# Layer-norm statistics from accumulators: row sums where the residuals are written, squares in one pass of ScalarE

## The reference

```
def _layernorm(x, axis=-1, eps=1e-05):
    m = jnp.mean(x, axis=axis, keepdims=True)
    v = jnp.var(x, axis=axis, keepdims=True)
    return (x - m) / jnp.sqrt(v + eps)

x = x + _L0_xattn_ref(_layernorm(x), ctx, ctx)        # autocorrelation by FFT, 9 best lags
x = x + _L0_ffn_ref(_layernorm(x), ...)               # dense 1024x1024 + low-rank experts, 2 of 8
x = x + _L1_xattn_ref(_layernorm(x), ctx, ...)        # windowed attention, 8 heads, window 16
x = x + _L1_ffn_ref(_layernorm(x), ...)               # low-rank experts, 2 of 4
```

## Time and profile before

| | |
|---|---|
| time, median of 3 runs | 2359.71 us (2359.32 to 2360.57) |
| span of the profiled execution | 2357.6 us |
| what lies around the span (median less span) | 2.1 us |
| busy: PE, DVE, ACT, POOL | 84%, 85%, 53%, 42% of the span |
| granted clock of TensorE, mean | 0.918 of full speed |

### The profile page before, as it was taken

How to read it: one execution, slowest core, us unless ns; L and a number is a source line. 1 busy time by engine, 2 the same in 40 slices (tenths; PEclk the granted TensorE clock), 3 DMA queues, 4 the chain that set the end, 5 groups by cost and what they waited for, 6 DMA issues and landing times.

```text
span 2357.6 us, 50630 instructions
## 1 busy us (share of the span) xinstructions
PE 1982.8 (84%) x18912; PEld 1159.5 (49%) x18912; DVE 2012.7 (85%) x5613; ACT 1246.3 (53%) x1795; POOL 994.9 (42%) x582
## 2 busy tenths in 40 slices
PE   5688888988888988888888888888888898888875
PEld 2355444555544555544555544555544555544543
DVE  5788889888889888898888898888888988898863
ACT  3255555455555455554555555455555555555543
POOL 1354434344434434444435444435434435434431
PEclk7899999999999999999999999999999999999985
DMA  5011110011110010111010111011111011111000
GB/s 195 10 37 37 45 44 31 22 44 36 44 44 35 18 44 36 44 44 40 13 44 36 44 44 44 9 44 36 44 44 44 9 44 36 44 44 36 9 10 19
DMA packets 24735, 91.58 MB, mean 39 GB/s; under 512 B 3137, under 2 KB 3265, under 8 KB 24577
## 3 DMA queue, kind: packets, MB, share of 16 engines
q1 hardware_dynamic: 24704, 91.17, 10.9%
HBM read 74.39 MB, written 16.78 MB: 39 GB/s over the span
## 4 chain that ended last, share of the span: by engine, by line
PE 38%; DVE 25%; issue 17%; ACT 10%; POOL 9%; DMA 0%; DVEq 0%; POOLq 0%; SPq 0%; ACTq 0%
PE pa L433 12%; PE pb L433 5%; PE pb L531 4%; PE pc L626 4%; PE pc L600 3%; POOL p_hl L1366 3%; POOL rest L1354 3%; POOL sc L1409 3%; DVE small L1118 2%; PE pc L433 2%; PE pb L536 2%; ACT v_pad L770 2%; DVE small L935 2%; DVE sc L1070 2%; DVE sc L1139 2%
## 5 line engine op out<-in xcount | busy, mean ns | idle before, releaser
L531 PE MATMUL pb<-w_base_h,even_words 128*128 128x512 f16 x1024 | 341.1, 396 | 0.4 <-ACT mid_t L712 0.4
L1409 POOL TENSOR_TENSOR sc<-sc,sc_rec 128x512 f32<-128x512 f32 x128 | 134.1, 1047 | 349.7 <-DVE sc_rec L1148 349.7
L1359 POOL TENSOR_TENSOR rest<-rest,v_im 128x1024 f32<-128x1024 f32 x32 | 75.6, 2363 | 453.4 <-DVE v_im L1031 453.4
L1366 POOL TENSOR_TENSOR p_hl<-sc,p_hl 128x512 f16<-128x512 f32 x128 | 191.1, 1493 | 161.6 <-ACT p_hl L712 161.6
L433 PE MATMUL pa<-ctx_a,tab 128*128 128x512 f32 x384 | 243.0, 767 | 16.8 <-DMA par<-in_parity 8.4
L433 PE MATMUL pa<-xn_a,tab 128*128 128x512 f32 x384 | 189.4, 617 | 43.4 <-ACT xn_a L712 43.4
L804 ACT ACTIVATE q_diag<-sc,par 32x1024 f32<-32x1024 f32 x192 | 215.9, 1140 | 9.7 <-DVE sc L1070 7.4
L600 PE MATMUL pc<-sc_t,v_diag 128*128 128x32 f16 x6144 | 174.0, 177 | 54.6 <-ACT rows_c L712 54.6
L600 PEld LDWEIGHTS pc<-sc_t,v_diag 128*128 128x128 f16 x6144 | 168.1, 97 | 89.5 <-ACT rows_c L712 60.5
L531 PE MATMUL pb<-w_base_l,even_words 128*128 128x512 f16 x512 | 201.2, 393 | 0.0
L712 ACT ACTIVATE rows_c<-pc 64x256 f32<-64x256 f32 x256 | 96.2, 376 | 183.9 <-PE pc L600 180.8
(11 more groups left out here) (141 smaller groups left out, 5357.8 us busy)
## 6 DMA issues: line engine op xcount, KB each, us to landing
x_a<-in_x SPq DMA_DIRECT2D x32, 512.0 KB, 3.3
ctx_a<-in_ctx_in SPq DMA_DIRECT2D x32, 512.0 KB, 3.3
x_res<-in_x SPq DMA_DIRECT2D x32, 512.0 KB, 3.9
ctx_b<-in_ctx_in SPq DMA_DIRECT2D x32, 512.0 KB, 4.1
out<-rows_c SPq DMA_DIRECT2D x32, 512.0 KB, 2.9
v_diag<-in_base_w SPq DMA_DIRECT2D x1, 4096.0 KB, 14.3
tab<-in_spectra SPq DMA_DIRECT2D x1, 576.0 KB, 5.1
q_diag<-in_ra SPq DMA_DIRECT2D x1, 544.0 KB, 15.2
```

The source lines that it names most:

```text
L531: mm(pb[:, h, :], rows[:, cols], weights[:, j, h * HALF:(h + 1) * HALF], start=(j == 0 and m == 0), stop=False)
L1366: g_.tensor_tensor(part[:, :, :, LO], sc[:, g % 2, :, :], part[:, :, :, HI], ALU.subtract)\
L1409: g_.tensor_tensor(sc[:, g % 2, :, :], sc[:, g % 2, :, :], sc_rec[:, blocks].unsqueeze(2).to_broadcast([P, GB, KEYS]), ALU.mult)\
```

## The change

Norm 0 keeps `bn_stats` and `bn_aggr`. For norms 1, 2 and 3 the operation that writes the residual also accumulates the sum of each row (for norm 1 a tensor_tensor becomes a scalar_tensor_tensor for that). VectorE turns that sum into the mean (`mean`, one 128x1 operation). ScalarE gets a new operation, `spread`: Square over all 1024 columns with the row sum as bias and a scale of -D, so that it squares (sum - D x), and an accumulator output that is D^2 times the sum of squared deviations. Its elementwise result goes to the place that the normalised rows will overwrite (xn_b or xn_c) and is not used. `root` k = 0 then waits for ScalarE (`ln_sq`) and not for VectorE's own `ln_mv`. The six `bn_stats` and three `bn_aggr` of these norms go. A memset of 128x1, with which the kernel holds back an operation of VectorE until a semaphore has come, goes before each of the three `bn_aggr` too.

```
+            def spread(b, n, rows, rows_out, place):
...
+                act.wait_ge(rows_out.sem, rows_out.after(b))
+                nc.scalar.activation(place[:, :], rows[:, :], ACT.Square, bias=ln_sum[n][:, :], scale=-float(D),
+                                     accum_out=mv[n][:, 1:2]).then_inc(ln_sq[n].sem, 1)
...
                     c_attended(c, 3)
+                if do_b:
+                    spread(b, 2, x_b, x2_out, xn_b)
                 if do_a:
                     a_values_long(i, 1)
...
                     a_transposed(i, 0)
                     a_transposed(i, 1)
+                if do_c:
+                    spread(c, 3, rows_c, x3_out, xn_c)
                 if do_b:
                     b_values(b)
...
                     b_value_blocks(b, 0, 1)
+                if do_a:
+                    spread(i, 1, x_b, x1_out, xn_b)
+                if do_b:
                     b_value_blocks(b, 0, 2)
...
+            def mean(b, n, rows_out):
+
+                dve.wait_ge(rows_out.sem, rows_out.after(b))
+                v.tensor_scalar(mv[n][:, 0:1], ln_sum[n][:, :], 1.0 / D, None, ALU.mult).then_inc(ln_mean[n].sem, 1)
...
                 if k == 0:
-                    dve.wait_ge(ln_mv[n].sem, ln_mv[n].after(b))
-                    v.tensor_scalar(var, mv[n][:, 1:2], 1e-5, 4.0 * RSQRT_K ** 6, ALU.add, ALU.mult)\
-                        .then_inc(steps.sem, 1)
+                    dve.wait_ge(ln_sq[n].sem, ln_sq[n].after(b))
+                    v.tensor_scalar(var, mv[n][:, 1:2], 4.0 * RSQRT_K ** 6 / D ** 3, 1e-5 * 4.0 * RSQRT_K ** 6,
+                                    ALU.mult, ALU.add).then_inc(steps.sem, 1)
...
-                v.tensor_tensor(x_b[:, :], pa_lo, x_res[:, :], ALU.add).then_inc(x1_out.sem, 1)
-
-
-            def b_norm(b, n, before):
-                dve.wait_ge(before.sem, before.after(b))
-                layer_norm(b, n, x_b)
+                v.scalar_tensor_tensor(out=x_b[:, :], in0=pa_lo, scalar=1.0, in1=x_res[:, :], op0=ALU.mult,
+                                       op1=ALU.add, accum_out=ln_sum[1][:, :]).then_inc(x1_out.sem, 1)
...
-                                       op0=ALU.mult, op1=ALU.add).then_inc(x2_out.sem, 1)
+                                       op0=ALU.mult, op1=ALU.add, accum_out=ln_sum[2][:, :]).then_inc(x2_out.sem, 1)
...
-                                       op0=ALU.add, op1=ALU.add).then_inc(x3_out.sem, 1)
-
-            def c_norm(b):
-                dve.wait_ge(x3_out.sem, x3_out.after(b))
-                layer_norm(b, 3, rows_c)
+                                       op0=ALU.add, op1=ALU.add, accum_out=ln_sum[3][:, :]).then_inc(x3_out.sem, 1)
...
                 if do_b:
-                    b_norm(b, 1, x1_out)
-                    variance(b, 1)
+                    mean(b, 1, x1_out)
...
                     b_base(b)
-                    b_norm(b, 2, x2_out)
-                    variance(b, 2)
+                    mean(b, 2, x2_out)
...
                     c_attention_residual(c)
-                    c_norm(c)
-                    variance(c, 3)
+                    mean(c, 3, x3_out)
```

More of the change, by code:

```diff
@@ L221, in build @@
         mid_t = [sb(f"mid_t{n}", [[P, E1 * RANK][n], P]) for n in range(2)]
-        bn = [little(2, 6) for n in range(4)]
+        bn = little(2, 6)
         mv = [little(2) for n in range(4)]
+        ln_sum = [little(1) for n in range(4)]
         rs_v = [little(1) for n in range(4)]
@@ L258, in build @@
         out_done = signal("out_done", 16)
-        ln_bn = [signal(f"ln_bn{n}", 2) for n in range(4)]
+        ln_bn = signal("ln_bn", 2)
         ln_mv = [signal(f"ln_mv{n}") for n in range(4)]
+        ln_mean = [signal(f"ln_mean{n}") for n in range(4)]
+        ln_sq = [signal(f"ln_sq{n}") for n in range(4)]
         ln_rs = [signal(f"ln_rs{n}", RSQRT_STEPS) for n in range(4)]
@@ L749, in a_transposed @@
                 copy(wt[:, h * HALF:(h + 1) * HALF], pa[:, 2 + h, :]).then_inc(wt_out.sem, 1)
+            def spread(b, n, rows, rows_out, place):
+                if n == 1:
+                    if not first(b):
+                        act.wait_ge(mm_qq.sem, mm_qq.after(b - 1))
+                elif n == 2:
+                    act.wait_ge(tr_x[0].sem, tr_x[0].after(b))
+                else:
+                    act.wait_ge(pt_out.sem, pt_out.after(b))
+                act.wait_ge(rows_out.sem, rows_out.after(b))
+                nc.scalar.activation(place[:, :], rows[:, :], ACT.Square, bias=ln_sum[n][:, :], scale=-float(D),
+                                     accum_out=mv[n][:, 1:2]).then_inc(ln_sq[n].sem, 1)
             def b_features(b, h):
@@ L930, in _, with a_variance @@
             v = nc.vector
[L932 to L939, removed]
+            def a_variance(b):
+                dve_wait(dve, ln_bn, ln_bn.after(b))
+                v.bn_aggr(mv[0][:, :], bn[:, :, :]).then_inc(ln_mv[0].sem, 1)
+            def mean(b, n, rows_out):
+                dve.wait_ge(rows_out.sem, rows_out.after(b))
+                v.tensor_scalar(mv[n][:, 0:1], ln_sum[n][:, :], 1.0 / D, None, ALU.mult).then_inc(ln_mean[n].sem, 1)
             def root(b, n, k):
@@ L946, in root @@
                 steps = ln_rs[n]
+                if k == 0 and n == 0:
+                    dve.wait_ge(ln_mv[0].sem, ln_mv[0].after(b))
+                    v.tensor_scalar(var, mv[0][:, 1:2], 1e-5, 4.0 * RSQRT_K ** 6, ALU.add, ALU.mult)\
+                        .then_inc(steps.sem, 1)
+                    return
                 if k == 0:
-                    dve.wait_ge(ln_mv[n].sem, ln_mv[n].after(b))
-                    v.tensor_scalar(var, mv[n][:, 1:2], 1e-5, 4.0 * RSQRT_K ** 6, ALU.add, ALU.mult)\
-                        .then_inc(steps.sem, 1)
+                    dve.wait_ge(ln_sq[n].sem, ln_sq[n].after(b))
+                    v.tensor_scalar(var, mv[n][:, 1:2], 4.0 * RSQRT_K ** 6 / D ** 3, 1e-5 * 4.0 * RSQRT_K ** 6,
+                                    ALU.mult, ALU.add).then_inc(steps.sem, 1)
                     return
@@ L969, in normalise @@
             def normalise(b, n, rows, place):
+                if n > 0:
+                    dve.wait_ge(ln_mean[n].sem, ln_mean[n].after(b))
                 dve.wait_ge(ln_rs[n].sem, ln_rs[n].after(b))
@@ L976, in a_norm @@
                 dve.wait_ge(x_in.sem, x_in.after(b))
-                layer_norm(b, 0, x_a)
+                for h in range(2):
+                    v.bn_stats(bn[:, h, :], x_a[:, h * HALF:(h + 1) * HALF]).then_inc(ln_bn.sem, 1)
             def a_norm_rows(b):
@@ L1220, in step @@
                 if do_next:
-                    variance(i + 1, 0)
+                    a_variance(i + 1)
                 if do_c:
@@ L1302, in _ @@
             a_norm(0)
-            variance(0, 0)
+            a_variance(0)
             for k in range(RSQRT_STEPS):
```

## The result

The changed kernel takes 2428.85 us (2427.37 to 2429.54, 4 runs) beside 2359.52 us for the kernel before: a ratio of 1.0293, 95% interval 1.0279 to 1.0308. It is slower, by 69 us. The prediction said 2431, range 2408 to 2456.

The account below looks back on a forecast made before the run. No engine alone bounds: the chain of waits does, with VectorE's k_l and TensorE level before the values. Span 2357.6 + stall 62 + step 32's 1 + clock 10 + 2.1 around = 2432.7, rounded down to 2431; range 2408 to 2456.

Parts of the forecast that it names:

- the place that decides: Norm 3: its Square stands behind k_h and xn_a on ScalarE, so root k = 0 starts 2.08 us late.
- The stall: VectorE stands 3.4 us behind residual 3, waiting for norm 3's Square; 62 us (54 to 74) for 30 steps.
- the shift of the values: TensorE's values start late behind k_l, by the same 2.08 us per step as root k = 0 of norm 3.
- Step 32: Near the end, without block A: ScalarE comes to the Square earlier, so the cost is 1 us.
- Norms 1 and 2: Norm 1 at the step's start: cost 0; norm 2 behind residual 2: VectorE gains 0.15 us, nothing gained or lost overall.
- One sign named for a right forecast: No idle time of more than 1.5 us released by the Squares of norms 1 and 2.
- The clock term: TensorE's gap before the values: half clock in ten of thirty steps, up to 1.37 us each, some 10 us (0 to 41).
- The stall without further clock loss: Rival: VectorE's wait at norm 3 costs 63 us and TensorE's clock holds, 2423 us; chance 0.32.
- the clock falls in nearly every step: Rival: TensorE drops to half clock behind the new gap nearly everywhere, 104 us more, 2464; chance 0.08.
- ScalarE would not be late: Rival: norm 3's Square is read before 1231.88, a faster kernel, 36 us at full effect, 2324; chance 0.05.
- later waits would take the stall up: Rival: the 2.08 us at norm 3 are absorbed, time within 0.2% (4.7 us); chance 0.06.
- activation tables would be loaded: Rival: Square and Exp exchange tables on ScalarE, four loads of 1.28 us per step, 111 us more, 2543; chance 0.02.

Follow-up runs that it names:

- the doubled Square: The change with the Square of norm 3 done twice on ScalarE, first into an unused tile: 2504.78 us, ratio 1.0615 against the kernel before.

## Why the prediction was right

**The place and the mechanism.** The step called the place that decides is as forecast: VectorE stands behind residual 3 until ScalarE has done k_h, xn_a and the Square, and k_l and the values follow late. The stall was 3.38 us (3.4 forecast), the shift of the values 1.95 us (2.08), 58 us in thirty steps where the sum has 62. Step 32 was priced at 1 us, and the end of the span came 1.1 later. The Square cost 1.16 us (1.14) and its read 0.21 (0.15), but both start some 0.1 us before what precedes them ends, so that root k = 0 followed the end of xn_a by 1.17 us and not by 1.33. Moving the wait behind k_l gave 59 to 62 us back.

**Norms 1 and 2.** Both at no cost or gain, as forecast. For norm 1 the first exponential still waits 0.65 us for VectorE, behind the copies that follow the Square:

```profile
1158.60 0.63 ACT L836 ACTIVATE sc<-sc 128x512 f32<-128x512 f32 x1 [0.65 <-DVE sc L1167]
```

One sign named for a right forecast did not come: no Square of norms 1 and 2 was to release an idle time of more than 1.5 us, but VectorE waits 1.85 us for that of norm 2. It costs nothing. Against the product from xn_a (1232.76 in the earlier trace rows, now 1126.19) root k = 0 of norm 2 starts 0.19 us earlier than before and residual 3 0.16 earlier; 0.15 and at most 0.1 were forecast. That the steps of norms 1 and 2 alone last what they lasted before is in the windows above.

**The clock term was wrong.** I gave it 10 us, ten stretches at half clock behind the new gap. The gap was 1.85 us and not 2.0, the clock stayed at 1.00 behind it in 29 of 30 steps, and the term measured some 1 us: 1.99 per step less 1.95. The error lay in placing a gap of 2.0 midway between 1.41 and 2.28 and pricing it so. The mechanism exists, and the doubled Square showed it at 2.89 us: 47 us.

**A term was missing.** I named what is queued behind the new waits in the loop, but not in step 0, where the Square of norm 1 stands ahead of the split of the weights: 7.1 us. The clock term 9 us too high, the stall 4 too high and the start 7 too low partly cancel, so it is luck that 2431 lies 2 us from the time; by its terms the sum was right to about 10 us.

**The rivals.** "The stall without further clock loss" was nearest in its mechanism, nearer than the forecast itself; its 2423 lacks the start. That the clock falls in nearly every step did not come: it fell in one of thirty. That ScalarE would not be late, that later waits would take the stall up, and that activation tables would be loaded are all excluded by the timeline after.

## What to carry to other kernels

Before work moves to an engine that is less busy, look at what that engine does at that moment and what the waiting engine has queued behind the result; an order in which due work stands before the wait costs nothing and was worth 62 us here. Look through the first and the last steps too, where the same program meets other work. A saving off the chain is worth nothing: 4 us of VectorE per step gave 0 to within 3 us in all, and moving 1.3 us out of the chain gave 39 us in all.

## What the runs showed of the hardware

The accumulator of an activation is read by an instruction of its own on ScalarE, 186 and 208 ns in the mean for the two forms, which starts about 0.1 us before the activation ends. The accumulator output on VectorE's residuals cost a read of 77 to 83 ns and changed their length by nothing (1.18 us before and after for residual 1).

TensorE's granted clock went with the length of a gap, but not with that alone: behind 1.85 us it stayed at the full level in 29 of 30 steps, behind 2.89 it was at the lower one, and behind one and the same gap of 1.63 us among narrow matmuls it fell in some steps and stayed in others. The two kernels with norm 3 by bn_stats and norms 1 and 2 moved lay some 17 us, 0.7%, above the sum of their parts, and the windows over their steps put this down to the clock. Four runs of one and the same kernel differed by 12 us, their mean clock going along, so a difference of that size between two kernels of this kind may be no more than that.
